# A two-layer graph network on one core: which step scores a ranked tile, and behind which gathers its y is scattered

## The reference, cut to what matters

```python
N, D = 8192, 128                      # adj: 8192 x 8192 of 0/1, denser towards low node numbers
# layer 0: attention over each node's neighbours
h = relu(layernorm(x));  H = h @ W.T + b;  s = H @ a_s;  r = H @ a_r
e = leaky_relu(A * s + A * r.T, 0.2)
x = x + softmax(where(A > 0, e, -9e15), axis=1) @ H
# layer 1: sum over neighbours, then maximum over neighbours
h = relu(layernorm(x)) @ weight
p = relu(adj @ h + bias)
x = x + (max over the neighbours j of row i of p[j])
```

## Time and profile before

| what | us |
|---|---|
| median of 3 runs (2621.01 to 2623.65) | 2622.08 |
| the profiled execution's own time | 2613.49 |
| its span | 2611.7 |
| DVE busy in it | 1495.5 (57%) |
| POOL busy | 1420.8 (54%) |
| PE busy | 1286.9 (49%) |
| ACT busy | 464.7 (18%) |

### The profile page before, as it was taken

How to read it: one execution, slowest core, us unless ns; L and a number is a source line. 1 busy time by engine, 2 the same in 40 slices (tenths; PEclk the granted TensorE clock), 3 DMA queues, 4 the chain that set the end, 5 groups by cost and what they waited for, 6 DMA issues and landing times.

```text
span 2611.7 us, 18582 instructions
## 1 busy us (share of the span) xinstructions
PE 1286.9 (49%) x5093; PEld 672.1 (26%) x5093; DVE 1495.5 (57%) x3498; ACT 464.7 (18%) x1561; POOL 1420.8 (54%) x1465
## 2 busy tenths in 40 slices
PE   3764245635243636533556996951532212475046
PEld 1441024413132313322442442420211101232013
DVE  6988757967343625437155553544757754883234
ACT  1641134502122403451440000000000000000000
POOL 0012655562755463568536556357757775567763
PEclk8987567867576767765777998975776555787568
DMA  9999848789674879842343222114212321222221
GB/s 357 404 375 413 279 146 297 292 281 356 219 299 141 312 275 398 334 158 56 95 130 90 60 78 67 28 50 89 51 46 68 91 76 36 55 53 51 72 69 44
DMA packets 161754, 443.40 MB, mean 170 GB/s; under 512 B 31986, under 2 KB 90661, under 8 KB 128750
## 3 DMA queue, kind: packets, MB, share of 16 engines
q1 hardware_dynamic: 78974, 307.90, 31.0%
q0 software_dynamic: 49360, 108.63, 16.6%
q10 hardware_dynamic: 33312, 25.63, 3.2%
HBM read 404.00 MB, written 37.98 MB: 169 GB/s over the span
## 4 chain that ended last, share of the span: by engine, by line
another core or an unknown queue 21%; PE 20%; DVE 16%; issue 14%; POOL 11%; DMA 7%; ACT 6%; SPq 5%; ACTq 0%; DVEq 0%; POOLq 0%
PE psV L1211 10%; DMA a_buf<-in_adj 6%; POOL ring L759 6%; POOL rec_all L759 5%; PE psV L1038 3%; SPq L480 2%; PE psH L1094 2%; ACT ring L851 2%; SPq L493 2%; PE psV L1232 2%; DVE a_buf L1677 2%; DVE a_buf L1680 1%; DVE trec L1485 1%; DVE V L1670 1%
## 5 line engine op out<-in xcount | busy, mean ns | idle before, releaser
L685 POOL DMA_INDIRECT ring<-h_table,srec x505 | 493.9, 978 | 280.7 <-issue 150.9
L1038 PE MATMUL psV<-a_buf,bit_ident 128*128 128x512 bf16 x1024 | 320.7, 479 | 215.5 <-DMA a_buf<-in_adj 155.2
L759 POOL DMA_INDIRECT rec_all<-p_table,srec x325 | 321.8, 990 | 184.4 <-issue 98.2
L1232 PE MATMUL psV<-a_buf,trec 128*128 128x512 f32 (+1 forms) x398 | 235.4, 746 | 249.4 <-issue 126.3
L1211 PE MATMUL psV<-rec_all,a_buf 128*128 128x512 bf16 x888 | 212.0, 393 | 51.1 <-issue 50.6
L1094 PE MATMUL psH<-ring,ident 128*128 128x128 f32 x1010 | 162.6, 324 | 142.6 <-issue 100.6
L1038 PEld LDWEIGHTS psV<-a_buf,bit_ident 128*128 128x128 bf16 x1024 | 116.0, 116 | 402.6 <-issue 292.5
L718 POOL DMA_INDIRECT ring<-y_table,srec x191 | 185.0, 969 | 60.9 <-issue 60.6
L1094 PEld LDWEIGHTS psH<-ring,ident 128*128 128x128 f32 x1010 | 154.4, 237 | 155.0 <-issue 145.3
L1232 PEld LDWEIGHTS psV<-a_buf,trec 128*128 128x128 f32 x398 | 94.5, 245 | 386.6 <-issue 243.2
L1232 PE MATMUL psH<-a_buf,trec 128*128 128x512 f32 x124 | 79.9, 778 | 216.5 <-issue 116.6
(11 more groups left out here) (258 smaller groups left out, 2296.2 us busy)
## 6 DMA issues: line engine op xcount, KB each, us to landing
a_buf<-in_adj SPq DMA_DIRECT2D x256, 1024.0 KB
ring<-h_table,srec POOLq DMA_INDIRECT x505
trec<-records ACTq DMA_DIRECT2D x63, 128.0 KB
packed<-wbuf ACTq DMA_DIRECT2D x28, 256.0 KB
a_buf<-packed SPq DMA_DIRECT2D x7, 1024.0 KB
rec_all<-p_table,srec POOLq DMA_INDIRECT x325
h_table<-stage POOLq DMA_DIRECT2D x16, 258.0 KB, 8.1
a_buf<-r_row SPq DMA_DIRECT2D x1, 4096.0 KB
```

The source lines that it names most:

```text
L685: pool.indirect_dma_start(ring[:, A_AT[q] + j, :], None, h_table, bass.IndirectOffsetOnAxis(srec_u[g][:, i, LIST + j:LIST + j + 1], 0)).th ...
L759: pool.indirect_dma_start(ring[:, at + j, 0:D] if at < RING else side[:, at - RING + j, :], None, p_table, bass.IndirectOffsetOnAxis(slot, ...
L1038: last = pe.matmul(psV[n % 2][:, h * BANK:(h + 1) * BANK].rearrange("p (g n) -> p g n", n=P), bit_ident[:, k, :], rows[:, :, k, :], start= ...
L1232: pe.matmul(psO[b % len(psO)][:, 0:width], results[:, n % RESULTS, :], hot[:, c % HOT, at:at + width], start=(ranked_tile(n) == FIRST[g]), ...
```

## The change

Only the two tables differ; no instruction is added to a tile or taken from it. Both tables, cut to their first lines:

```diff
-STEP = [18, 19, 20, 20, 21, 22, 22, 23, 24, 24, 25, 25, 26, 26, 27, 27, 34, 38, 40, 41, 42, 43, 44, 45, 46, 46,
...
+STEP = [18, 19, 20, 20, 21, 22, 22, 23, 24, 24, 25, 26, 26, 27, 27, 28, 33, 38, 39, 40, 41, 43, 43, 46, 46, 47, 50, 53, 54, 54, 55, 55, 57, 57, 58, 58, 59, 60, 60, 61, 61, 62, 62, 63, 63, 64, 64, 66, 67, 68, 68, 69, 69, 70, 70, 71, 71, 72, 72, 73, 73, 74, 74]
...
-BEHIND = [5, 6, 8, 8, 9, 11, 11, 12, 14, 14, 16, 16, 17, 17, 17, 17, 20, 21, 23, 24, 25, 26, 27, 27, 30, 30, 31,
...
+BEHIND = [5, 6, 9, 9, 9, 10, 10, 11, 14, 14, 16, 16, 17, 17, 17, 17, 20, 21, 23, 24, 25, 26, 27, 27, 29, 30, 31, 33, 33, 35, 36, 36, 37, 38, 40, 40, 41, 45, 45, 47, 47, 47, 47, 49, 49, 50, 51, 52, 53, 56, 57, 59, 59, 59, 59, 60, 62, 62, 62, 62, 62, 62, 62]
```

More of the change, by code:

```diff
@@ L129 @@
 C_COUNT = [a + b for a, b in zip(gather_counts(C_SLOTS), C_BASE * NC)]
-STEP = [18, 19, 20, 20, 21, 22, 22, 23, 24, 24, 25, 25, 26, 26, 27, 27, 34, 38, 40, 41, 42, 43, 44, 45, 46, 46,
-    47, 53, 54, 55, 55, 56, 57, 57, 58, 58, 59, 60, 60, 61, 61, 62, 62, 63, 63, 64, 64, 65, 66, 67, 68, 68,
-    69, 69, 70, 70, 71, 71, 72, 72, 73, 73, 74]
-BEHIND = [5, 6, 8, 8, 9, 11, 11, 12, 14, 14, 16, 16, 17, 17, 17, 17, 20, 21, 23, 24, 25, 26, 27, 27, 30, 30, 31,
-    32, 33, 35, 35, 36, 38, 38, 40, 40, 41, 44, 44, 47, 47, 47, 47, 49, 49, 51, 51, 52, 53, 54, 56, 56, 58,
-    58, 61, 61, 62, 62, 62, 62, 62, 62, 62]
+STEP = [18, 19, 20, 20, 21, 22, 22, 23, 24, 24, 25, 26, 26, 27, 27, 28, 33, 38, 39, 40, 41, 43, 43, 46, 46, 47, 50, 53, 54, 54, 55, 55, 57, 57, 58, 58, 59, 60, 60, 61, 61, 62, 62, 63, 63, 64, 64, 66, 67, 68, 68, 69, 69, 70, 70, 71, 71, 72, 72, 73, 73, 74, 74]
+BEHIND = [5, 6, 9, 9, 9, 10, 10, 11, 14, 14, 16, 16, 17, 17, 17, 17, 20, 21, 23, 24, 25, 26, 27, 27, 29, 30, 31, 33, 33, 35, 36, 36, 37, 38, 40, 40, 41, 45, 45, 47, 47, 47, 47, 49, 49, 50, 51, 52, 53, 56, 57, 59, 59, 59, 59, 60, 62, 62, 62, 62, 62, 62, 62]
 HUB_SCORES, HUB_SUMS, HUB_NORM = T, T + 4, T + 8
```

## The result

The change makes the kernel slower: 2644.4 us median (2630.8 to 2660.0, 12 runs) against 2615.3 us of the kernel before in the same series (2607.9 to 2623.7, 12 runs), a ratio of 1.0108, 95% interval 1.0080 to 1.0136, some 28 us. The forecast was 2597, with 2638 as the upper end. The twelve times stand in two clusters: six from 2630.8 to 2636.5, six from 2652.3 to 2660.0. The kernel before has one. The profiled execution is of the upper cluster: its own time is 2652.28, its span 2650.5, 38.8 us over the span of before.

The account below looks back on a forecast made before the run. The prediction saw no single bounding engine: work is handed from engine to engine, and y's last scatter decides. Terms 0 - 11 + 0 - 7 + 0 - 7 = -25 us off 2622.1 gave 2597 (2575 to 2612; eight in ten, 2562 to 2638).

Parts of the forecast that it names:

- Group 0: Steps 18 to 28: later scores of q11, q13, q15 cost or gain nothing; 0, between -1 and +1 us.
- q16 at step 33: Scoring q16 one step earlier starts q17's gathers and sum, and steps from 40 on, earlier; -11 us (0 to -22).
- q18 to q22: q18 to q20 one step earlier, q21 and q22 together at 43: gains and stalls cancel; 0 (-43 to +40).
- q23 to q26: Steps 44 to 47: two waits for sums, 10.3 us, go and some 3 us return; -7 us (0 to -16).
- the stretch goes: Rival: steps 42 and 43 were stretched by their own chain of single tiles, not gathers; 2567 us, chance 0.12.
- the stretch grows: Rival: the unbroken gathers of q20 to q24 stretch two more steps from 10 to 30 us; 2637 us, chance 0.24.
- Group 2: q29 and q31 fill other steps of two, the sums between remain; 0 us, between -5 and +5.
- Group 3: From step 65 one tile later: hub exponents begin 11.8 us earlier, about 5 given back; -7 us (-11.8 to +2).
- The slower rival: Same as "the stretch grows": +40 us from POOL's unbroken gathers of q20 to q24; 2637 us, chance 0.24.
- the point from which it decides: Where POOL, no longer held by sums, runs ahead for more than 36 us, the slower rival decides.
- Rule and row: By the skill's rule, gathers don't stretch step 43 and one unbroken run costs nothing; PE's 23.45 us wait doesn't settle it.

Follow-up runs that it names:

- f4: The change with STEP of group 0 (q0 to q15) put back and BEHIND kept: 2655.4 us, ratio 1.0148 to the kernel before.
- g3: The kernel before with BEHIND alone of q0 to q15 as in the change: ratio 1.0112 to the kernel before.
- h2: The change with two BEHIND numbers put back (q2 and q3 scattered behind q8): ratio 1.0085 to the kernel before, +22 us.
- f3: The change, with POOL starting q16's gathers only when q15 has been closed, slower kind of chip: 2648.4 us, ratio 1.0095 to the kernel before.
- g2: The change, with POOL waiting after every 8 gathers of a ranked tile until they have landed: ratio 1.0083 to the kernel before.
- f1: The change itself, unedited, measured again on another chip of the slower kind: 2667.3 us, ratio 1.0174 to the kernel before.
- h1: The kernel before with two BEHIND numbers changed (q2 and q3 scattered behind q9 instead of q8): ratio 1.0037, +10 us.
- e1: The kernel before with group 0's entries (q0 to q15) of both tables as in the change: 2633.8 us, ratio 1.0083, +22 us.
- f2: The kernel before with q15 scored at step 28 instead of 27, slower kind of chip: 2624.7 us, ratio 1.0023.
- e2: The kernel before with group 1's entries (q16 to q26) of both tables as in the change: ratio 0.9998.
- g4: The kernel before with group 2's entries (q27 to q46) of both tables as in the change, slower kind of chip: ratio 1.0023.
- e4: The change with group 0's entries of both tables put back as before: ratio 1.0040 to the kernel before, +10.5 us.
- e3: The kernel before with group 3's entries (q47 to q62) of both tables as in the change: ratio 0.9999.
- e6: The kernel before with BEHIND alone of q0 to q15 as in the change, on the faster chip: ratio 1.0011.
- e8: The change, with POOL starting q16's gathers only when q15 has been closed, on the faster chip: ratio 0.9984 to the kernel before.
- e5: The kernel before with q15 scored at step 28 instead of 27, on the faster chip: ratio 1.0008.

## Why the prediction was wrong

**What the traces say together.** The 16 traces from the slower kind of chip (those of before and of the change, and 14 experiments) fall into two sets. Ten have a pause of 1.25 to 2.35 us ahead of group 1's rank scatters. In these the gathers of q16 begin 4.0 to 6.5 us after step 29, and the trace shows no wait of DVE in steps 28 and 29. Six have none (0.30 us). In four (the change, f4, g3, h2) the gathers begin 6.2 to 9.0 us before step 29, and a wait of 34 to 43 us follows. The other two are those in which POOL was made to wait (f3) or to pause (g2), and the wait is absent. So one near-tie, whether DVE's ranks or POOL come first, decides over a wait of some 40 us, of which some 20 to 25 reach the end by the distance of the change's two clusters. (The rest is not lost, since the kernel before has waits in that run as well: PE waits 28.9 us for its tile there.) The change's profile, from the upper cluster, has the wait; f1's, from the lower, has not. h1 and g3 differ only in q5, q6 and q7, and g3 has tipped: moving these three tips the tie. It doesn't do so each time (e1's and f1's profiled executions have them moved and keep the pause), and they were never moved alone. Scattering q2 and q3 behind q9, with its run of 22 issues, adds 10 us in the median.

**Term by term.**

- *Group 0: 0 (-1 to +1).* This step failed. It says "POOL's gathers and scatters keep their number", and prices nothing for their places. Measured +22 for all of group 0 (e1), and, each on another chip, +10 for q2 and q3 behind q9 alone (h1) and +29 for all of BEHIND without the steps (g3). The step of q15, of which the term spoke, costs 6 us (0 to 12, f2). A scatter moved past seven gathers was visible in the diff, and the earlier trace rows had shown that the other engines stand still inside long runs; the prediction weighed that for group 1 only.
- *q16 at step 33: -11 (0 to -22).* The first half was right and the gain 0. The score came 11.0 us and the gather 9.2 us earlier (e2), but the sum of q17 didn't follow: step 38 now began at the end of a 10 us wait inside the run of gathers, and the score of q17 came 20.6 us later than before. "The beginning of the sum and the end of the gathers lie 1 us apart" holds wherever group 1's order is the old one (the sum begins 0.1 to 3.9 us before the run's end in all seven such traces without pauses), but it is not a tie that moves with the gathers: in the seven with the new order the sum begins 10.6 to 14.7 us after the run's end, since DVE's score comes late. The term's own bound of 0, "if the sum hangs on something else", was the case. In the change itself ACT's raw scores of q16 exist at 601.17, DVE scores at 634.16, and the sum is waited for 14.39 us.
- *q18 to q22: 0 (-43 to +40)* and *q23 to q26: -7.* Together with the term above, 0.0 (-5 to +3) in e2's runs. The long wait of step 43 went (step 43 is 10.1 us long in the change) and came back in steps 41 and 42, 39.7 and 32.7 us: "the stretch goes" and "the stretch grows" both happened and cancelled. The 7 us never reached POOL: step 46 of e2 begins 0.6 us later than before.
- *Group 2: 0 (-5 to +5).* +6 us (-1 to +13) in g4's times, which agrees with e4's +10.5 on top of groups 1 and 3 at 0 each but isn't clear of 0. The traces are clearer. In all seven with group 2's entries and no pauses, 9.3 to 16.2 us are lost between the beginnings of steps 46 and 62 (9.3 in the change's, 10.6 in g4's and e4's); in the six without these entries it is -8.3 to +4.3. So this term was some 10 us too low as well, and the change's loss has a second part in it. Which of its entries costs this isn't shown.
- *Group 3: -7 (-11.8 to +2).* The first half was right: ACT's first exponent comes 53.75 us after the first chunk (55 was forecast; 66.6 before). All of it is given back (e3's times allow anything within 4 us of 0), and by the traces more: counted from step 62, the last scatter comes 2.5 to 6.4 us later than before in seven of the eight traces with group 3's entries (1.6 us earlier in the change's own), and -0.9 to +1.7 in the seven experiments without them. The change's tail:

```profile
1213.29 0.74 DVE L1504 TENSOR_SCALAR V<-a_buf,rs_col 128x1024 f32<-128x1024 f32 x1
...
1267.04 1.15 ACT L890 ACTIVATE a_buf<-a_buf,hub_neg 128x1024 f32<-128x1024 f32 x1 [12.43 <-DVEq L1517]
...
1278.15 0.17 DVE L1466 SCALAR_TENSOR_TENSOR e_sc<-e_sc 128x8 f32<-128x8 f32 x1 [11.18 <-issue]
...
1304.40 0.17 DVE L1466 SCALAR_TENSOR_TENSOR e_sc<-e_sc 128x7 f32<-128x7 f32 x1 [21.15 <-ACT e_sc L831]
...
1384.76 0.16 DVE L1466 SCALAR_TENSOR_TENSOR e_sc<-e_sc 128x3 f32<-128x3 f32 x1
...
1403.14 0.96 POOL L691 DMA_INDIRECT y_table<-trec,srec  x1 [0.30 <-issue]
```

From the first chunk the score of step 68 comes at 64.9 us (77.7 before), but the next at 91.1, since DVE waits 21.15 us there (17.07 before); the last scores stand at 171.5 (176.2 before), and the last scatter 18.4 us behind them (13.0 before). That last 5 us was forecast. The 8 us lost in steps 68 to 73 weren't: that these steps have "two ranked tiles each, as before" is true, but it didn't keep them from growing.

**The rivals.** The slower rival had the right kind of cause (handovers stand still while POOL issues without a pause) and by chance the right sign and size (2637), but its place was wrong: q20 to q24 cost nothing at the end (e2), and "the point from which it decides" was in group 0. The chance of 0.24 was too low mainly because group 0 wasn't considered among its places.

**Rule and row.** The Trainium skill, SBUF — State Buffer, section "Who interferes with whom", says that DMA never contends with a compute engine. In f3 and g2 no data, no amount of DMA and no dependency among PE, ACT and DVE is changed, only when POOL issues, and the wait of 34 to 43 us on those three, which the four unguarded traces with the gathers ahead of step 29 all have, is absent. The rule isn't refuted, since no run shows which resource is held; but as a reason to price a run of gathers at zero it fails here.

**What stays open.** What holds the engines' signals back inside such a run, and why four chips show it and one doesn't. How late the signals are is in the records: in the kernel before, 11 of the 25 signals of PE's sums between 380 and 1000 us are recorded over 0.5 us after the sum's end, up to 21.8 us; on the fifth chip all 41 of e6 come within 0.02 us. PE's ends are modelled by the profile, so that for PE the work itself may have been late; for ACT's L861 above it was the signal. They don't wait for the end of the run in every case. After f1's run of 22 the signal comes 1.0 us after the run's end; DVE goes on 6.9 us after the end of q16's run in the change, 7.1 in h2 and 2.8 in g3, but 2.9 us before it in f4, and at 788.6 in the kernel before, inside a run that went on until 822.6. One rival can be set aside, a wait for instructions: the queues that fetch them have no packet between 541.9 and 596.2 in the change's trace, and the engines go on at 592.2. Open too is which entry of group 2 costs its part. No version measured is faster than the kernel before on the slower kind of chip; the change with e8's wait was 0.16% faster (0.04 to 0.27) on the faster one, and 0.95% slower on the other.

## What to carry to other kernels

When a table moves DMA issues past others in an engine's list, count the longest unbroken run of issues before and after it, and look for near-ties (a wait of 1 or 2 us) behind it: here 1.9 us of pause decided over 20 to 25. A time that comes in two clusters where the old one had one may point to such a tie, and two profiles, one of each cluster, can name it, as they did here. A gain found in front of a long, unexplained wait should be priced at zero until something shows what ends that wait.

## What was not expected of the hardware

- The same kernel takes 2615 to 2624 us on four chips and 2264 us on a fifth, with the same work: DVE is busy 1495.5 us and POOL 1420.8 in the profile of before (2613.5 us), 1497.1 and 1419.9 in that of e5 (2261.0 us), which differs from it only in the step of q15. The granted clock is 0.73 and 0.77. Common standstills of PE, ACT and DVE of over 5 us are no measure of the difference: up to 1200 us they sum to 81 us in before and 66 us in e5. What the traces show to differ is how soon a signal follows the work: 0.02 us at most for the sums on the fifth chip, up to 43 us on the others, and DVE's waits between its own instructions of `extract`: none in e5 to e8, 34 in before (such as 1.1, 1.0 and 3.1 us from 554 to 561, inside POOL's run). How much of the 350 us this makes isn't shown.
- PE's matmul records can end 42.5 us before the signal that belongs to them is recorded: the sum of q15 at 549.72 and 592.20. The wait of 6 us in step 27 is of the same kind: the sum ended at 513.19, its signal is recorded at 526.15.
- A wait of 5.4 to 6.2 us of DVE in step 27 goes with a faster read-back of the ranked records (3.3 to 3.6 us of POOL's wait instead of 7.6 to 9.0). The tile stream rests meanwhile: during the read-back the DMA share is 0.40 in the change and 1.01 before. That the one causes the other isn't shown, but e6, which has no such wait and a share of 1.02, needs 8.1 us. Together the two move the engines apart by some 11 us.
